# The filter of a group is transformed inside the group ahead of it, in the middle stage of an FFT long-convolution layer

## The reference

```
proj = layernorm(x) @ in_proj_w + in_proj_b       # three branches; only v and the last are used
v    = conv3(proj[..., 0]) + short_b              # 3 taps along the positions
h    = (filter network of the positions)          # 2048 x 512, one filter for all batches
conv = irfft(rfft(v, n=4096) * rfft(h, n=4096))[:2048]
y    = x + (proj[..., 2] * conv) @ out_w + out_b
out  = y + layernorm(y) @ (weighted sum of 8 adapters) + bias
```

## Time and profile before

| | |
|---|---|
| three runs of the kernel before | 2394.57, 2400.53, 2400.60 us; median 2400.53 |
| the profiled execution | 2403.85 us |
| its span | 2402.0 us |
| PE / DVE / POOL / ACT busy | 96% / 64% / 39% / 35% of the span |
| `middle`, first to last matmul | 1009.5 to 1417.8 us of the span |
| DMA traffic | 496.6 MB, mean 207 GB/s |

### The profile page before, as it was taken

The page is one execution under the profiler, slowest core; times in us unless marked ns, Lnnn a source line. Parts: engine busy times, 40 slices in busy tenths (PEclk is TensorE's granted clock), DMA queues, the critical chain, the costliest instruction groups (busy, mean ns, idle before and its releaser), DMA issues.

```text
span 2402.0 us, 39735 instructions
## 1 busy us (share of the span) xinstructions
PE 2315.6 (96%) x12804; PEld 1624.1 (68%) x12804; DVE 1530.5 (64%) x2180; ACT 843.9 (35%) x1152; POOL 933.0 (39%) x1182
## 2 busy tenths in 40 slices
PE   6689999999999999999999979999999999999998
PEld 2267777777777777644444426777777777777776
DVE  5534444443434444367777757888888888888886
ACT  3234444444444444344444432222222222222222
POOL 2122222222222222100000026777777777777774
PEclk9889999999999999999999999999999999999999
DMA  5545545555444546589999997766665665666563
GB/s 187 181 137 159 196 140 179 162 164 196 150 162 146 188 160 221 205 312 359 356 353 355 362 358 229 246 178 176 176 180 175 179 175 176 178 179 177 177 179 101
DMA packets 180517, 496.60 MB, mean 207 GB/s; under 512 B 19419, under 2 KB 19740, under 8 KB 159332
## 3 DMA queue, kind: packets, MB, share of 16 engines
q1 hardware_dynamic: 150756, 395.10, 51.4%
q10 hardware_dynamic: 29696, 100.68, 11.6%
HBM read 276.27 MB, written 219.43 MB: 206 GB/s over the span
## 4 chain that ended last, share of the span: by engine, by line
PE 53%; DVE 2%; issue 2%; DMA 1%; ACT 0%; DVEq 0%; POOL 0%; POOLq 0%; SPq 0%
PE m_psW L1030 7%; PE m_psA L1013 6%; PE b_psF L183 5%; PE b_psC L1328 5%; PE b_psF L184 5%; PE b_psO L184 5%; PE b_psF L185 5%; PE b_psO L183 5%; PE b_psO L185 5%; PE b_psP L1342 2%; PE b_psT L1359 2%; DVE m_m L1101 2%; DMA spec<-wide_out 0%; DMA b_fin<-spec 0%; DVE b_o L1397 0%
## 5 line engine op out<-in xcount | busy, mean ns | idle before, releaser
L1101 DVE TENSOR_TENSOR m_m<-m_psA,m_spec 128x1024 f32<-128x1024 f32 x256 | 295.5, 1215 | 114.8 <-PE m_psA L1013 113.1
L758 POOL TENSOR_TENSOR vl<-v,vh 128x512 fp32r<-128x512 f32 x128 | 165.2, 1291 | 390.1 <-ACT vh L716 390.1
L1292 ACT ACTIVATE b_zh<-b_psT 128x512 fp32r<-128x512 f32 x128 | 76.5, 597 | 636.9 <-PE b_psT L1359 636.9
L1030 PE MATMUL m_psW<-m_m,mats 64*64 64x512 f32 x2048 | 256.0, 591 | 2.5 <-issue 2.5
L1013 PE MATMUL m_psA<-m_xin,mats 64*64 64x512 f32 x1536 | 212.9, 601 | 9.5 <-DVE m_m L1101 5.9
L183 PE MATMUL psV<-wvh,nth 128*128 128x512 f32 x512 | 213.6, 417 | 0.6 <-DVE ntl L840 0.6
L859 DVE TENSOR_TENSOR gto<-psG,bgr 128x512 f32<-128x512 f32 x128 | 87.5, 684 | 195.4 <-PE psG L185 195.2
L183 PE MATMUL b_psO<-woh,b_oh 128*128 128x512 f32 x512 | 211.8, 414 | 0.0
L183 PE MATMUL b_psF<-wfh,b_zh 128*128 128x512 f32 x512 | 207.7, 406 | 2.8 <-DVE b_zl L1421 2.8
L840 DVE TENSOR_TENSOR ntl<-psT,nth 128x512 fp32r<-128x512 f32 x128 | 88.1, 688 | 178.9 <-ACT nth L710 178.9
L184 PE MATMUL b_psO<-wol,b_oh 128*128 128x512 f32 x512 | 201.4, 393 | 0.0
(11 more groups left out here) (136 smaller groups left out, 4685.3 us busy)
## 6 DMA issues: line engine op xcount, KB each, us to landing
spec<-wide_out SPq DMA_DIRECT2D x64, 1024.0 KB, 9.0
spec<-wide_out ACTq DMA_DIRECT2D x64, 1024.0 KB, 9.2
b_fin<-spec SPq DMA_DIRECT2D x128, 512.0 KB, 4.6
m_xin<-spec SPq DMA_DIRECT2D x30, 2048.0 KB, 11.7
xg<-in_L_attn_x_dram SPq DMA_DIRECT2D x64, 512.0 KB, 6.2
gate_d<-gto SPq DMA_DIRECT2D x32, 1024.0 KB, 4.0
b_gin<-gate_d SPq DMA_DIRECT2D x128, 256.0 KB, 3.6
b_xin<-in_L_attn_x_dram SPq DMA_DIRECT2D x256, 128.0 KB, 3.2
```

What stands on the lines that cost most here:

```text
L758: pool.tensor_tensor(vl[:, t % 2], v[:, t % 2], vh[:, t % 2].bitcast(F32), ALU.subtract).then_inc(v_lo, 1)
L1030: mm = pe.matmul(psW[pair % 2][half[slot], q, :], ws[slot][half[q]], m[half[q], pair % RM, part, slot, :], start=part == 0, stop=part == 1)
L1101: dve.tensor_tensor(m[:, (k - 2) % RM, part], psA[k % RA][:], spec[:, par, part], ALU.mult).then_inc(m_done, 1)
```

## The change

In `middle` the six steps are ordered anew: `PAIR_AT = (0, 1, 3, 5)` are pairs, `FILTER_AT = (2, 4)` are the two filter products of the next group. The first group's filter products stand ahead of the loop; the last group makes none. All inverses follow two steps behind. A group's filter rows have a semaphore of their own (`filter_in`) and are loaded as soon as the slot is free; the 8 batches are loaded in two halves of 1 MB. The four `edge_a` loads become two, and the 28 edge loads of `back` become 14 of double size, each for two tiles.

```
+            PAIR_AT = (0, 1, 3, 5)
+            FILTER_AT = (2, 4)
 load:
-                    sp.wait_ge(a_ps, (group(i, s) - 1) * PAIRS)
-                    sp.dma_start(xin[:, par, B], rows_of(spec_f, group(i, s))).then_inc(x_in[par], 16)
-                    sp.dma_start(xin[:, par, 0:B], rows_of(spec1, group(i, s))).then_inc(x_in[par], 16)
+                    sp.wait_ge(f_ps, 2 * g - 2)
+                    sp.dma_start(xin[:, par, B], rows_of(spec_f, g)).then_inc(mc["filter_in"][par], 16)
+                    for k in range(2):
+                        batches = slice(k * B // 2, (k + 1) * B // 2)
+                        sp.wait_ge(a_ps, 4 * g - 6 + 2 * k)
+                        sp.dma_start(xin[:, par, batches], rows_of(spec1, g)[:, batches]).then_inc(x_in[k][par], 16)
 forward (PE), a pair:
+                        if pair == 0:
+                            pe.wait_ge(f_done, 2 * g + (1 if first else 2))
+                        elif pair == 1 and first:
+                            pe.wait_ge(f_done, 2)
+                        else:
+                            pe.wait_ge(m_done, 8 * g + (0, 0, 4, 6)[pair])
+                        pair_products(g, par, pair, data_first if first else data_w, psA[k % RA])
 forward, a filter part:
+                    if isinstance(g, int) and g == GROUPS - 1:
+                        return
+                    if part == 0:
+                        (wait for filter_in of the next group)
+                        pe.wait_ge(m_done, 8 * g + 2)
+                    else:
+                        pe.wait_ge(f_done, 2 * g + 3)
+                    filter_products(1 - par, (same_w, cross_w)[part], psA[k % RA])
-                pipelined(pe, GROUPS // 2, S, [(forward, 0), (inverse_early, 2), (inverse_last, 3)])
+                pe.wait_ge(mc["filter_in"][0], 16)
+                filter_products(0, same_first, psA[0])
+                filter_products(0, cross_first, psA[1])
+                pipelined(pe, GROUPS // 2, S, [(forward, 0), (inverse, 2)])
 ACT:
-                pipelined(act, GROUPS // 2, S, [(spectrum, 0), (out_early, 2), (out_last, 3), (w_high, 3)])
+                pipelined(act, GROUPS // 2, S, [(spectrum, 0), (out_copy, 2), (w_high, 3)])
 back, load_edges (t even only):
-                        sp.dma_start(edge(q, t), edge_f[q][:, t * C:(t + 1) * C]).then_inc(edge_in[t], 16)
+                        sp.dma_start(edge_b[:, t - EARLY:t - EARLY + 2, q],
+                                     edge_f[q][:, t * C:(t + 2) * C].rearrange("p (t c) -> p t c", t=2)).then_inc(edge_in[t // 2], 16)
```

More of the change, by code:

```diff
@@ L898, in middle @@
             low = sem("m_low")
-            x_in = [sem(f"m_x_in{i}") for i in range(2)]
+            x_in = [[sem(f"m_x_in{k}{i}") for i in range(2)] for k in range(2)]
             last_in = [sem(f"m_last_in{i}") for i in range(2)]
@@ L922, in pair_no @@
             def pair_no(i, s):
[L923 removed]
+                return group(i, s) * PAIRS + PAIR_AT.index(s % GS)
             def at_first(i, s, groups=1):
@@ L985, in _, with pair_products @@
                 pe.wait_ge(mc["mats_in"], 16)
[L987 to L1009, removed]
+                def pair_products(g, par, pair, w, ps_a):
                     pe.sem_inc(passed, 1)
@@ L1012, in forward @@
                         for slot in range(KG):
-                            mm = pe.matmul(psA[k % RA][half[q], slot, :], w[half[slot]],
-                                           xin[half[slot], par, B if k < 2 else 2 * (k - 2) + q, :], start=True, stop=True)
-                    mm.then_inc(f_ps if k < 2 else a_ps, 1)
+                            mm = pe.matmul(ps_a[half[q], slot, :], w[half[slot]], xin[half[slot], par, 2 * pair + q, :],
+                                           start=True, stop=True)
@@ L1017, in inverse @@
                 def inverse(i, s):
-                    pair = s % GS - 2
+                    k = s % GS
+                    if k not in PAIR_AT:
+                        return
+                    pair = PAIR_AT.index(k)
                     n = pair_no(i, s)
@@ L1048, in spectrum @@
                     k = s % GS
-                    if k >= 2:
+                    g = group(i, s)
+                    if k not in FILTER_AT or isinstance(g, int) and g == GROUPS - 1:
                         return
[L1051 to L1055, removed]
+                    part, par = FILTER_AT.index(k), 1 - s // GS
+                    act.wait_ge(f_ps, 2 * g + part + 3)
+                    if not at_first(i, s):
+                        act.wait_ge(m_done, 8 * g)
+                    act.activation(spec[:, par, part], psA[k % RA][:], ACT.Copy).then_inc(f_done, 1)
                 def out_copy(i, s):
-                    par, pair = s // GS, s % GS - 2
+                    if s % GS not in PAIR_AT:
+                        return
+                    par, pair = s // GS, PAIR_AT.index(s % GS)
                     n = pair_no(i, s)
@@ L1083, in w_high @@
                         act.activation(bc["woh"][:], wraw[:], ACT.Copy).then_inc(high, 1)
-                pipelined(act, GROUPS // 2, S, [(spectrum, 0), (out_early, 2), (out_last, 3), (w_high, 3)])
+                for part in range(2):
+                    act.wait_ge(f_ps, part + 1)
+                    act.activation(spec[:, 0, part], psA[part][:], ACT.Copy).then_inc(f_done, 1)
+                pipelined(act, GROUPS // 2, S, [(spectrum, 0), (out_copy, 2), (w_high, 3)])
             @block.vector
@@ L1090, in product @@
                     par, k = s // GS, s % GS
-                    if k < 2:
+                    if k not in PAIR_AT:
                         return
+                    pair = PAIR_AT.index(k)
                     n = pair_no(i, s)
@@ L1100, in product @@
                             dve.wait_ge(w_ps, n - RM + 1)
-                        dve.tensor_tensor(m[:, (k - 2) % RM, part], psA[k % RA][:], spec[:, par, part], ALU.mult).then_inc(m_done, 1)
+                        dve.tensor_tensor(m[:, pair % RM, part], psA[k % RA][:], spec[:, par, part], ALU.mult).then_inc(m_done, 1)
                 pipelined(dve, GROUPS // 2, S, [(product, 0)])
@@ L1191, in load_edges @@
                 def load_edges(b, t):
-                    if not (isinstance(b, int) and b == 0) or t < EARLY:
+                    if not (isinstance(b, int) and b == 0) or t < EARLY or t % 2:
                         return
@@ L1463, in hyena_adapter_kernel @@
             "mats_in": sem("m_mats_in"), "early_in": [sem(f"m_early_in{i}") for i in range(2)],
+            "filter_in": [sem(f"m_filter_in{i}") for i in range(2)],
         }
```

55 lines of the change are left out of this document (35 added, 20 removed).

## The result

The changed kernel takes 2403.18 us (median of 14 runs), the kernel before 2398.34 (14 runs beside them): a ratio of 1.0022, 95% interval 1.0014 to 1.0029, so **3.4 to 7.0 us slower**, 4.8 by the medians. 11.4 were forecast. The direction was right and the size twice too large: the change ends within 0.3%. The profiled execution took 2407.27 us, its span is 2405.2.

What follows compares the result with a forecast made beforehand. The prediction took PE's matmuls plus one PSUM loop with DVE as the bound, not DMA. The median of 2400.5 us plus 11.4 for the later store, other terms at 0, gave 2412 us, range 2404 to 2420.

Steps and rivals of the forecast that it cites:

- What bounds the kernel: Middle stage: 12.04 us of PE matmuls plus a 0.43 us gap from one PSUM loop per 12.47 us group; DMA keeps up.
- Two loops in place of one: New order in the middle stage: one wait goes, waits of 0.38 us before F3 and F1 come; period 12.84 us.
- The price of a loop: Middle stage, from an F to the next F writing the same PSUM tile: 1.32 + 2.36 + 0.15 = 3.83 us.
- +11.4 to the store: Last group's store of pairs 0 and 1: 11.7 us later from the longer periods, less 0.3, so 11.4 us late.
- The bound of 3.75: Lower limit of the PSUM loop's length in us; 3.75 to 3.95 meant 0.30 to 0.50 us a group.
- Fs+ follows F0 without a gap: Next group's first filter matmul after pair 0's: 3.82 us apart from the gap before F1, so no wait.
- a third loop: Rival, chance 0.09: another 0.1 to 0.2 us wait per group between F0 and Fs+, +3 to +6 us, 2417.
- The loads at 0: Middle stage's split data and filter loads: slack gained where no load is short, so 0 us.
- The handover at 0: Middle to back stage: `fin` issued 9.1 instead of 11.4 us later, up to 2.7 slower; about 0, bounds -2 and +5.
- The stop that may move: Middle stage's start, PE's code arriving late beside 2 MB loads: 6.4 us kept, so 0, bounds -6.4 and +5.
- The edges: Back stage's merged edge loads: 1.4 us more before the first release, covered by 4.1 us; 0, bounds -1 and +1.

Runs made afterwards that it cites:

- light_loads: The kernel before with each data load cut from 8 batches to 2, 0.5 MB for 2 MB: 2395.07 us, ratio 0.9989.
- half_all: Old order with half an inverse moved from behind F3 to behind F1, plus the changed kernel's loads: 2383.18 us, ratio 0.9937 to the kernel before.
- old_a_last: Old order with the changed loads, DVE waiting last for PE's product semaphore: 2390.77 us, ratio 0.9959 to the kernel before.
- same_before: The kernel before profiled once more, unchanged: 401.61 us from the middle stage's first matmul to the last group's first store, period 12.47 us.
- all_but_order: The changed kernel with the old order of PE, ACT and DVE, keeping its loads and merged edges: 2394.13 us, ratio 0.9978 to the kernel before.
- new_w_high: The changed kernel with ACT's w_high two steps behind and ahead of the copies: 2404.23 us, ratio 1.0028 to the kernel before.
- same_new: The changed kernel profiled once more, unchanged: 408.23 us from the middle stage's first matmul to the last group's first store, period 12.72 us.

## Why the prediction was right or wrong

- **What bounds the kernel: right.** Matmuls plus one open loop, not DMA. light_loads shows it for the rows' 0.98 of DMA share, and half_all moves 368 GB/s for 200 us.
- **Two loops in place of one: right**, at the two places named, before F3 and before F1.
- **The price of a loop: the step that failed.** It was taken as 3.83 us from F0 and F1 of the old order and applied to F2 and F3. There it is 3.71 and 3.67. I weighed that it might be shorter with DVE idle and put it aside with "in the old order DVE was idle before P0 and the loop was no shorter": but P0 is the one product with two register instructions behind its wait, so the row that I used against a shorter loop was the exception. That F1 to P1 also took 1.32 made both rows agree; old_a_last shows that this one too was long for its register instruction, as it falls to 1.13 with DVE busy just as shortly before. 0.8 of gaps became 0.64, and 0.38 a group became 0.25: 30 x 0.13 = 3.9 us of the 4.8 by which +11.4 to the store exceeds the measured +6.6; the other 0.8 is what same_before lost in its last turn. The bound of 3.75 was too high as well.
- **Fs+ follows F0 without a gap: wrong.** That hung on a gap of 0.38 before F1. With 0.21 there, 0.16 opened before Fs+. The rival "a third loop" happened, for another reason, and inside a smaller sum.
- **The loads at 0: wrong.** They give back 3 to 8 us by the runs (all_but_order). I asked whether a load was waited for within a period, and it was not; the gain lies outside the periods. I put a 0 there from what is waited for, without a row on how long a backlog takes to drain. What makes the gain is shown only in part: 0.8 to 2.2 us of it are in the handover. That part the changed kernel pays away again: its handover keeps 14.5 us, as `low` now comes late, and new_w_high gets 1.0 of it back. Against the runs' +4.8 the forecast was 6.6 too high: 3.9 for the loop's price, the rest for this term less what the order costs outside its periods.
- **The handover at 0: right in its sum**, and in its parts: `fin` issued 2.3 us less late than the store (9.70 to 7.36) and landing 1.9 us later (5.20 to 7.14); -2.3 and at most +2.7 had been given.
- **The stop that may move: right to leave at 0 with bounds, wrong in its nature.** That PE's code comes late was read rightly. But the long stop isn't a thing of the order, it comes and goes with the execution: gone in same_before and same_new.
- **The edges: right**, POOL's wait grew from 5.06 to 7.58 us and nothing followed.
- The median of 2403 lies just under the range's 2404, 8.8 us under the forecast's 2412. Of these, 6.6 are the change and 2.2 the starting point: 2400.5 was the median of three runs, and fourteen give 2398.3. From that the same range would have begun at 2402 and held the result, by luck in its bounds and not by its terms. With the loads' gain in it, it would have reached lower. The profile of before, at 3.3 us over its median, had a stop of over 2 us in it that 12 of the 16 profiles don't have.

## What to carry to other kernels

Price a loop through a buffer at the place where it will stand, and look there at the consumer's instructions between its wait and its work: in this kernel's hardware loop the wait was carried by register instructions that compute the next counts. Waiting last for the semaphore that comes last took 7 us off this kernel without moving any work. To close a PSUM loop, count the producer's work between two writes of one tile for every tile, and move work in pieces smaller than the gap needs; and take the load's slack into the sum, since a faster order uses it up.

## What the runs showed of the hardware

- One register instruction between a DVE wait and its tensor operation cost 0.06 to 0.10 us in the changed kernel, a met wait nothing visible: 1.15, 1.21 and 1.31 us with none, one and two. Where DVE had just ended its product before, in the old order, one cost 0.19 or 0.1 by the group's parity (1.32 against 1.13 and 1.21 in old_a_last).
- The first matmul of a stage came between 1003.2 and 1010.0 us of the span over sixteen profiles whose code ahead of it computes the same, and one stop of PE of 2 to 5 us, for no semaphore and until 1.0 to 1.5 us after the end of a 16 KB packet of its code, came in some executions of a program and not in others. A single profile can't price anything of that size; cutting each at the same events can.
- HBM and SBUF exchanged 368 GB/s for 200 us at a DMA share of 0.99. The Trainium skill, "DMA: Bandwidth & Descriptors", section "Where 436 GB/s comes from", has the memory side bind at about 358, half of what it gives for a stack with two cores; these rows, of one core that runs alone, go past it, with reads and writes mixed.
